# Dummy matmuls ahead of the first scores, and four small VectorE operations of each batch given to GpSimd

## The reference

```python
a_alpha = (t @ attn_alpha_w.T)[:, None, :]
x = x + a_alpha * _attention(_ada_rmsnorm(x, t, ...), W_q, W_k, W_v, W_o)      # 16 heads of 16, softmax
f_alpha = (t @ ffn_alpha_w.T)[:, None, :]
return x + f_alpha * _swiglu(_ada_rmsnorm(x, t, ...), gate_w, hidden_w, out_w, out_b)   # 1024 hidden
```

## Time and profile before

| | before |
|---|---|
| time, median of 3 runs | 748.71 us (748.31 to 750.13) |
| the profiled execution's own time | 747.71 us, of which its span is 745.9 us |
| PE busy | 642.7 us (86%) |
| DVE busy | 433.6 us (58%) |
| ACT busy | 392.8 us (53%) |
| POOL busy | 59.1 us (8%) |
| mean granted clock of TensorE | 0.929 of full speed |

### The profile page before, as it was taken

The page is one execution under the profiler, slowest core; times in us unless marked ns, Lnnn a source line. Parts: engine busy times, 40 slices in busy tenths (PEclk is TensorE's granted clock), DMA queues, the critical chain, the costliest instruction groups (busy, mean ns, idle before and its releaser), DMA issues.

```text
span 745.9 us, 9973 instructions
## 1 busy us (share of the span) xinstructions
PE 642.7 (86%) x3441; PEld 427.8 (57%) x3441; DVE 433.6 (58%) x860; ACT 392.8 (53%) x748; POOL 59.1 (8%) x89
## 2 busy tenths in 40 slices
PE   2755698799989989799989988799899988999896
PEld 0411477354468767544477777444478776543585
DVE  0451595688274655877364756886365737883344
ACT  1432477156864564257764564267755572368710
POOL 2010320300000002100000003000000004000000
PEclk9856799689999999899999999799999999699999
DMA  8997430521000005220000005220000013220000
GB/s 282 378 379 237 113 112 29 106 39 29 1 1 1 1 29 106 51 44 3 1 1 4 1 29 106 51 44 2 0 1 1 1 32 75 51 44 1 1 1 29
DMA packets 34483, 45.12 MB, mean 60 GB/s; under 512 B 4736, under 2 KB 27392, under 8 KB 34304
## 3 DMA queue, kind: packets, MB, share of 16 engines
q1 hardware_dynamic: 29728, 31.32, 15.0%
q0 software_dynamic: 3488, 10.49, 4.9%
q10 hardware_dynamic: 1216, 2.66, 1.4%
HBM read 28.45 MB, written 3.15 MB: 42 GB/s over the span
## 4 chain that ended last, share of the span: by engine, by line
PE 61%; DMA 11%; DVE 11%; ACT 10%; issue 4%; SPq 2%; ACTq 1%; DVEq 0%
PE psum L1215 28%; PE psum L1375 10%; PE psum L1437 7%; PE psum L1448 7%; DMA arena<-in_hyp_w 4%; DMA early_pieces<-in_hyp_w 3%; DVE mx L1032 3%; DMA kst<-split 2%; ACT arena L537 2%; PE psum L1476 1%; ACT kst L537 1%; ACT act L537 1%; PE psum L1303 1%; PE psum L1234 1%; PE psum L1337 1%
## 5 line engine op out<-in xcount | busy, mean ns | idle before, releaser
L714 ACT ACTIVATE arena<-psum 128x512 f32<-128x512 f32 x256 | 141.6, 600 | 89.6 <-PE psum L1437 88.5
L1032 DVE TENSOR_REDUCE mx<-psum 128x1 f32<-128x512 f32 x256 | 162.5, 683 | 41.9 <-PE psum L1375 41.6
L1375 PE MATMUL psum<-kst,qst 96*128 96x512 f32 x192 | 88.2, 511 | 20.7 <-DMA kst<-split 10.3
L1215 PE MATMUL psum<-act,ghw_hi 128*128 128x512 f32 (+1 forms) x288 | 89.6, 377 | 3.0 <-DVE act L833 2.5
L1437 PE MATMUL psum<-qst,kst 98*128 98x512 f32 x192 | 82.6, 452 | 1.9 <-ACT arena L714 1.3
L1375 PEld LDWEIGHTS psum<-kst,qst 96*128 96x128 f32 x192 | 43.0, 227 | 60.0 <-DVE mx L1032 35.6
L1215 PE MATMUL psum<-upw_hi,kst 128*128 128x512 f32 x256 | 71.3, 400 | 2.0 <-issue 1.5
L1448 PE MATMUL psum<-arena,vals 128*17 128x512 f32 x512 | 69.2, 613 | 1.3 <-ACT arena L714 1.0
L1215 PEld LDWEIGHTS psum<-act,ghw_hi 128*128 128x128 f32 x288 | 52.5, 190 | 15.3 <-DVE act L833 4.7
L434 POOL DMA_DIRECT2D kst<-split x36 | 17.7, 497 | 489.6 <-DMA kst<-split 407.6
L1215 PEld LDWEIGHTS psum<-upw_hi,kst 128*128 128x128 f32 x256 | 46.5, 189 | 11.7 <-issue 2.4
(11 more groups left out here) (184 smaller groups left out, 1079.9 us busy)
## 6 DMA issues: line engine op xcount, KB each, us to landing
early_pieces<-in_hyp_w SPq DMA_DIRECT2D x17, 512.0 KB, 9.3
arena<-in_hyp_w SPq DMA_DIRECT2D x15, 512.0 KB, 9.3
qst<-split SPq DMA_DIRECT2D x72, 64.0 KB, 3.4
kst<-split POOLq DMA_DIRECT2D x36, 128.0 KB, 3.5
arena<-in_up_w POOLq DMA_DIRECT2D x8, 256.0 KB, 5.4
arena<-in_x SPq DMA_DIRECT2D x4, 512.0 KB, 3.4
arena<-in_gh_w POOLq DMA_DIRECT2D x8, 256.0 KB, 3.6
out_x<-arena SPq DMA_DIRECT2D x8, 256.0 KB, 2.1
```

What stands on the lines that cost most here:

```text
L714: s.activation(probs[:, kb % 2, i, :], bank[3 + n % RING], ACT.Exp).then_inc(a_p, 1)
L1032: v.reduce_max(mx[:, g % 2, col:col + 1], bank[u % RING], AX.X).then_inc(d_max, 1)
L1215: ins = pe.matmul(dst, lhs(a, c), rhs(z, c), start=start and n == 0, stop=stop and n == len(terms) - 1, skip_group_check=skip)
L1375: pe.matmul(bank[u % RING], qst[g % 3][0:KROWS, i, P * t:P * t + P], keys_of(g)[0:KROWS, i // 2, :], start=True, stop=True).then_inc(e_max, 1)
```

## The change

It has two parts.

First, dummy matmuls (`keep_clock`, 128x128 weights, 512 columns). Ahead of the first maxima tile of a batch, once ACT has copied the values out of banks 5 and 6: 14 in batch 0, 6 in the others. In batch 0 also one behind each of the 21 maxima tiles of the ramp, and four ahead of the first score. In the other batches three ahead of maxima tile 20 (once DVE has read bank 4), one behind it, and two behind the last `kept_out`. That makes 39 in batch 0 and 12 in each other batch, 75 in all.

Second, work goes from DVE to GpSimd. The two additions of the kept sums (`kept_x4`) and the two alpha products (`alphas`) now stand at the end of GpSimd's `batch`, behind `stack_k(b, 3)`. Four places wait for them: SP's `results` (for the additions), ACT's copy of the first heads (`heads_copy`, whose target overlays `kept_z`), the use of `wo_alpha` on PE and that of `alpha_ob` on DVE. PE's first `weigh` waits for DVE's multiplication only.

```diff
@@ SP
-            def results(first_done, rows):
+            def results(added, first_done, rows):
                 for h in range(2):
-                    sp.wait_ge(d_outs, first_done + h)
+                    sp.wait_ge(added, first_done + h)
                     sp.dma_start(out[rows(h), :].rearrange("(t p) d -> p t d", p=P),
                                  x4_tok[:, 2 * h:2 * h + 2, :]).then_inc(out_done, 16)
...
                 if not first:
-                    results(b * 2 - 1, lambda h: bass.ds(b * L - L + h * HALF, HALF))
+                    results(p_kept_x4, b * 2 - 1, lambda h: bass.ds(b * L - L + h * HALF, HALF))
                 maxima_rows(b, 1)
                 stack_q(b, 3)
@@ GpSimd
+            def kept_x4(b, h):
+                pool.wait_ge(d_kept_ff, b * 2 - 1 + h)
+                pool.sem_inc(keys_free, 1)
+                pair = slice(2 * h, 2 * h + 2)
+                pool.tensor_tensor(x4_tok[:, pair, :], kept_z[:, pair, :], x4_tok[:, pair, :], ALU.add
+                                   ).then_inc(p_kept_x4, 1)
+            def alphas(b, first):
+                pool.wait_ge(d_alpha, b + 1)
+                pool.sem_inc(keys_free, 1)
+                pool.tensor_tensor(alpha_ob[:, :], alpha[:, D:2 * D], outb[:, :], ALU.mult).then_inc(p_alpha_ob, 1)
+                if first:
+                    pool.wait_ge(vow_in, 16)
+                pool.tensor_tensor(wo_alpha[:, :, :], vow[:, :, D:2 * D],
+                                   alpha[:, 0:D].unsqueeze(1).to_broadcast([P, C, D]), ALU.mult
+                                   ).then_inc(p_wo_alpha, 1)
...
                 stack_k(b, 3)
+                if not first:
+                    for h in range(2):
+                        kept_x4(b, h)
+                alphas(b, first)
@@ ACT, heads_copy
+                    if g == 0 and not first:
+                        s.wait_ge(p_kept_x4, b * 2)
@@ DVE, kept_output and alphas
-                v.wait_ge(d_kept_ff, b * 2 + h - 1)
-                v.tensor_tensor(x4_tok[:, pair, :], kept_z[:, pair, :], x4_tok[:, pair, :], ALU.add
-                                ).then_inc(d_outs, 1)
...
-                    v.tensor_tensor(alpha_ob[:, :], alpha[:, D:2 * D], outb[:, :], ALU.mult)
-                    if first:
-                        v.wait_ge(vow_in, 16)
-                    v.tensor_tensor(wo_alpha[:, :, :], vow[:, :, D:2 * D],
-                                    alpha[:, 0:D].unsqueeze(1).to_broadcast([P, C, D]), ALU.mult
-                                    ).then_inc(d_woalpha, 1)
@@ PE
+                pe.wait_ge(a_v, b * 2 + 2)
+                keep_clock(bank[6], 14 if first else 6)
                 for u in range(FIRST_MAX):
                     max_tile(u)
-                    if not first:
+                    if first:
+                        keep_clock(bank[6], 1)
+                    else:
...
+                    if u == FIRST_MAX - 2 and not first:
+                        pe.wait_ge(d_kept_hh, b * KEPT)
+                        keep_clock(bank[4], 3)
                     if u == FIRST_MAX - 1 and not first:
+                        keep_clock(bank[4], 1)
                         kept_out(2, range(T))
+                        keep_clock(bank[4], 2)
+                if first:
+                    keep_clock(bank[6], 4)
```

More of the change, by code:

```diff
@@ L230, in build @@
         x_first, hyp_rest = sem("x_first_in"), sem("hyp_rest")
-        d_woalpha = sem("dve_wo_alpha")
         d_held = sem("dve_held")
@@ L240, in build @@
         d_part = sem("dve_part_out")
-        p_kept_lo = sem("pool_kept_lo")
+        p_kept_lo, p_kept_x4 = sem("pool_kept_lo"), sem("pool_kept_x4")
+        p_alpha_ob, p_wo_alpha = sem("pool_alpha_ob"), sem("pool_wo_alpha")
         e_half = sem("pe_half")
@@ L402, in batch @@
                 if last:
-                    results(b * 2 + 1, lambda h: bass.ds(b * L + h * HALF, HALF))
+                    results(d_outs, 1, lambda h: bass.ds(b * L + h * HALF, HALF))
             batch(0, False, first=True)
@@ L961, in alphas @@
                     v.tensor_copy(alpha[:, :], bank[7]).then_inc(d_alpha, 1)
-                    v.wait_ge(d_alpha, b + 1)
-                    v.tensor_tensor(alpha_ob[:, :], alpha[:, D:2 * D], outb[:, :], ALU.mult)
-                    if first:
-                        v.wait_ge(vow_in, 16)
-                    v.tensor_tensor(wo_alpha[:, :, :], vow[:, :, D:2 * D],
-                                    alpha[:, 0:D].unsqueeze(1).to_broadcast([P, C, D]), ALU.mult
-                                    ).then_inc(d_woalpha, 1)
                 for t in range(T):
@@ L1112, in batch @@
                 v.wait_ge(d_x4, b * 2 + 2)
+                v.wait_ge(p_alpha_ob, b + 1)
                 v.tensor_tensor(x3_tok[:, :, :], x4_tok[:, :, :],
@@ L1445, in weigh @@
                     if kb == 0 and g == 0 and not first:
-                        pe.wait_ge(d_outs, b * 2)
+                        pe.wait_ge(d_kept_ff, b * 2)
                     for i in range(G):
@@ L1474, in attention_out @@
                         pe.wait_ge(a_onT, b * 3 + 1)
-                        pe.wait_ge(d_woalpha, b + 1)
+                        pe.wait_ge(p_wo_alpha, b + 1)
                     ins = pe.matmul(bank[1 + t // 2][:, D * (t % 2):D * (t % 2) + D], oT[:, c, P * t:P * t + P],
```

## The result

The changed kernel took 756.18 us (median of 6 runs, 754.54 to 757.22), the kernel before 749.08 us on the same chip (6 runs, 747.42 to 751.21). The ratio is 1.009 with an interval of 1.0069 to 1.0111: slower, by 7.1 us. The forecast was 754.5 us.

A forecast was written before the change was run, and what follows sets the result against it. PE, 61% of the chain, bounds the kernel through its waits and half-speed clock. Gains of 21.1 us (17.6 ramps, 3.5 alpha products) against a loss of 26.7 us: 5.6 us slower, 754.5 us, range 747 to 766 us.

The forecast's parts named there:

- the queue behind the outputs: Group 1's rows wait in SP's queue behind `results`, which waits for GpSimd's additions: 6.7 us lost in each of batches 1 to 3.
- Half speed behind the wait: Group 1 of batches 1 to 3 starts with PE at half speed for 5 us, costing 2.2 us each (1.4 to 3.4).
- The rival by which this speed is free: DVE and ACT might set the pace in group 1 while PE is slow: 747.7 us, no change; chance 0.14.
- Alpha products: Moved off DVE in group 1, they end PE's waits for maxima: 0.87 us gained in each of four batches, 3.5 us.
- The held clock in the ramps: Dummies keep PE at full speed in all four ramps; with the additions off DVE, 17.6 us gained in sum.
- the forecast's 1.2 us: In batch 1 `kept_out(2)` at full speed would release DVE sooner, which had idled 1.23 us for it: 1.2 us gained.
- a fall of the clock in the ramps: Sign that the prediction is wrong: the granted clock falls in the ramps, making the kernel slower still.
- the ten maxima: In batch 1's ramp, ten maxima taking 8.4 us would take 6.15 us at DVE's own pace: 2.3 us gained.
- The rival in which the ramp stays cold: Clock falls in batches 1 to 3 as before, leaving 1.4 of each batch's 4.9 us gain: 766 us; chance 0.13.

## Why the prediction was right, step by step

- **The step that decided, the queue behind the outputs: right, in place and size.** The chain from GpSimd's first transfer to the score took 7.11 us (323.07 to 330.18), forecast 7.3. Its terms: issues 1.50 and 1.50, additions 2.48 for 2.55, landing 1.8 to 1.9. Group 1 was held up by 6.4 to 6.5 us in each batch, forecast 6.7. Either end of the chain undone gives back 26 us.
- **Half speed behind the wait: right.** 2.1 us in each batch by the dummies in the wait, forecast 2.2. The stretch lasted 6.8 to 10.2 us, but part of it lies before the scores: in batch 1 it held 4.7 us from the first score on (330.18 to 334.9), where I had assumed 5. The rival by which this speed is free is out.
- **Alpha products: right in the mechanism.** 0.98 us in each batch against 0.87; they take 0.73 and 1.28 us on GpSimd, with nobody waiting.
- **The held clock in the ramps: the step that was off.** Its sum was 17.6 us and measured 13.7. The term in it that failed is that the dummies hold the clock through each ramp. In the changed kernel it still fell once in batch 1 and once in batch 3: in batch 1 PE came late to `kept_out(2)`, DVE idled 1.30 us for it (against 1.23), and the forecast's 1.2 us from there was not seen. In batch 0, where no such place exists, 1.42 us came of 1.5. The prediction had named a fall of the clock in the ramps as a sign against it, and two of the four ramps showed one.
- **The split within that sum was wrong too, and this hid in the total.** I had the additions worth 1.4 us and the dummies 2.3 us for the ten maxima. The additions are worth 2.7 to 2.9 us, since PE's stand behind them costs the clock as well; the dummies alone bring 5.6 us in the whole kernel. With no dummy at all the three ramps were 10.1 us shorter than before, where I had given the additions 4.2 us; with the dummies they were 12.3 us shorter. The rival in which the ramp stays cold and only 1.4 us of each 4.9 remain was therefore priced too dear: with no dummies at all it is 763.8 us and not 766.
- **The whole.** Gains 13.7 + 3.9 us, losses 19.4 + 6.3 us, and 0.95 us in the front: +9.1 us between the spans, forecast +5.6. Of the 3.5 us missed, 3.9 are the ramps', 0.95 the front's, and the other terms gave 1.4 back. The median, 756.18 us, lies only 1.7 us from the forecast, and that is in part luck: the two profiled executions differ by 2.0 us more than the medians do.

What stays open: why the row's issue and landing were slow when the outputs alone were late; why the front's length varies by up to 2.9 us between executions; and by what the clock stays up or falls in batches 1 and 2, whose programs are the same.

## What to carry to other kernels

Work handed to an idle engine is late by whatever stands ahead of it in that engine's order, and what it delays is whatever stands behind the one who waits for it. Follow both orders to the end before pricing the operation itself: here 2.5 us of additions cost nothing in one place, and 26 us over the kernel behind one more buffer wait. Price a stand of PE with the half speed behind it (6.4 us cost 8.5), and shorten the stand first: three dummies placed where PE has already waited held the clock in only 7 of 18 ramps. Eight spread ahead of that place held it in three of three, but that is one trace.

## What the runs showed of the hardware

The clock fell in stands much shorter than the 4.77 us of batch 0: behind one of 1.80 us, in a window where PE was busy 0.57 of 2.00 us, it went from 1.00 to 0.50. In batch 1 of the changed kernel it fell at 304.1, though PE had not stood for more than 0.44 us at a time since 300.3. Filling a stand of 6.4 us with 28 dummies held it at 1.00, and what followed was 2.1 us shorter. GpSimd's addition of 128x512 took 1.24 to 1.26 us against 0.69 on DVE, and DVE's maxima beside it kept their pace. An issue on SP that usually takes 0.59 us took 1.52 and 1.50 us in two batches, with GpSimd issuing in the same two microseconds, but 0.62 us in a third where GpSimd issued as well.
